# First and third attention: products of 512 constant columns that nobody reads, behind the phases of the delta rule

## What is computed

```python
q, k = l2norm(q), l2norm(k); v = v * beta; kb = k * beta
A = where(tri, 0, -(kb @ k^T))            # per chunk
inv = (I - A)^-1                          # reference: row by row
u, w = inv @ v, inv @ kb
for each chunk:                           # scan, state S
    u_adj = u - w @ S
    out = q @ S + where(strict, 0, q @ k^T) @ u_adj
    S = S + k^T @ u_adj
```

## Time and profile before

| | us |
|---|---|
| median of 3 runs | 5696.86 |
| lowest, highest | 5684.6, 5700.64 |
| profiled execution | 5712.86 |
| its span | 5711.5 |
| PE busy | 4092.1 (72%) |
| DVE busy | 3020.5 (53%) |
| ACT busy | 1912.4 (33%) |
| POOL busy | 816.5 (14%) |
| mean granted clock of PE | 0.761 of 2.4 GHz |

### The profile page before, as it was taken

One profiled execution on the slowest core, in us unless ns is written; L12 is line 12 of the kernel. 1 busy time (PEld: TensorE's weight loads), 2 busy tenths in 40 slices (PEclk: granted clock), 3 DMA queues, 4 the chain that ended last, 5 costly groups with the idle time before them and its releaser, 6 DMA issues.

```text
span 5711.5 us, 93833 instructions
## 1 busy us (share of the span) xinstructions
PE 4092.1 (72%) x39179; PEld 3175.9 (56%) x39228; DVE 3020.5 (53%) x8021; ACT 1912.4 (33%) x4196; POOL 816.5 (14%) x600
## 2 busy tenths in 40 slices
PE   6786969367777877774747668586777777776398
PEld 5674848255555655653536556474444555455277
DVE  4545363425554455556355665656666666665233
ACT  2233231223333333331232332324444555552122
POOL 0000000231111011101610000001212111110444
PEclk7555555588898998885766666668898998897599
DMA  9100000140000000001210000000000000000255
GB/s 271 46 2 1 2 1 2 59 157 1 1 1 1 1 1 1 1 1 36 28 43 2 1 1 2 1 3 1 1 1 1 1 1 1 1 1 17 72 160 143
DMA packets 140856, 152.26 MB, mean 27 GB/s; under 512 B 7809, under 2 KB 128003, under 8 KB 139793
## 3 DMA queue, kind: packets, MB, share of 16 engines
q1 hardware_dynamic: 119024, 128.21, 7.6%
q0 software_dynamic: 21408, 18.05, 1.9%
HBM read 87.38 MB, written 59.76 MB: 26 GB/s over the span
## 4 chain that ended last, share of the span: by engine, by line
PE 50%; DVE 29%; ACT 12%; issue 4%; POOL 2%; DMA 2%; another core or an unknown queue 1%; SPq 0%; DVEq 0%; POOLq 0%; ACTq 0%
PE banks_lane L801 4%; ACT work L3241 4%; PE banks_lane L422 3%; PE banks_lane L3678 2%; PE banks_lane L1881 2%; PE banks_lane L1242 2%; PE banks_lane L809 2%; PE banks_lane L3127 2%; PE banks_lane L935 2%; PE banks_lane L3162 1%; PE banks_lane L3149 1%; ACT work L1975 1%; DVE work L2796 1%; DVE weights L3251 1%
## 5 line engine op out<-in xcount | busy, mean ns | idle before, releaser
L422 PE MATMUL banks_lane<-constants,work 128*128 128x128 f32 x968 | 194.6, 346 | 453.2 <-DVE work L408 208.1
L422 PEld LDWEIGHTS banks_lane<-constants,work 128*128 128x128 f32 x968 | 146.2, 179 | 521.0 <-DVE work L408 195.6
L422 PE MATMUL banks_lane<-constants,weights 128*128 128x128 f32 x596 | 125.3, 347 | 355.7 <-DVE weights L408 93.3
L402 POOL TENSOR_TENSOR weights<-weights,constants 128x4 f32<-128x4 f32 x76 | 78.6, 1034 | 1974.0 <-DVE weights L397 1974.0
L422 PEld LDWEIGHTS banks_lane<-constants,weights 128*128 128x128 f32 x596 | 89.0, 179 | 389.9 <-issue 168.8
L3241 ACT ACTIVATE work<-banks_lane,weights 128x192 f32<-128x192 f32 (+1 forms) x512 | 249.4, 506 | 137.0 <-DVE weights L3338 137.0
L402 POOL TENSOR_TENSOR work<-work,constants 128x4 f32<-128x4 f32 x76 | 77.4, 1019 | 1193.6 <-DVE work L397 1193.6
L3345 POOL TENSOR_TENSOR weights<-weights,constants 128x16 f32<-128x16 f32 x64 | 185.5, 2898 | 377.6 <-DVE weights L3253 377.6
L3334 DVE TENSOR_REDUCE weights<-banks_lane 128x2 f32<-128x384 f32 (+1 forms) x256 | 122.4, 520 | 145.5 <-PE banks_lane L3149 145.5
L2028 DVE TENSOR_REDUCE work<-banks_lane 128x2 f32<-128x512 f32 x256 | 158.8, 683 | 67.6 <-PE banks_lane L1895 67.4
L3162 PE MATMUL banks_lane<-constants,work 128*128 128x128 f32 x896 | 136.1, 298 | 80.8 <-DVE work L3326 43.5
(11 more groups left out here) (773 smaller groups left out, 11034.4 us busy)
## 6 DMA issues: line engine op xcount, KB each, us to landing
work<-experts_dram_l_ffn SPq DMA_DIRECT2D x39, 964.0 KB
room_l_ffn<-work SPq DMA_DIRECT2D x30, 1188.0 KB, 14.2
work<-experts_dram_l_ffn SPq DMA_DIRECT2D x23, 512.0 KB
weights<-weights_dram SPq DMA_DIRECT2D x1, 4833.5 KB, 14.3
work<-room_l_ffn SPq DMA_DIRECT2D x36, 132.0 KB
weights<-weights_dram SPq DMA_DIRECT2D x1, 4112.0 KB, 12.6
weights<-bands_dram SPq DMA_DIRECT2D x1, 4096.0 KB, 13.7
weights<-room_l_ffn SPq DMA_DIRECT2D x26, 132.0 KB
```

The lines of the kernel that those rows point to most:

```text
L402: pool.tensor_tensor(n.rstd, n.rstd, c("neghalf", cols=(0, n.rstd.shape[1])), ALU.pow).then_inc(*u.pool.step(name))
L422: done = pe.transpose(bank[0:rows, t * P:(t + 1) * P], block, c("ident"))
```

## The change

`keep_busy` issues n products of "ident" with "later": 128 rows, 128 weight columns, 512 bfloat16 columns, start and stop set, into a whole bank of the unit's own lane. It increments no semaphore and waits for none. It is called

- at the entry of each unit, 8 times (`FILL_ENTRY`), behind L1062 in the first attention, behind the transpositions to rows in the third (there with a wait for ACT's `v_rows0`, so that b[0] has been read);
- behind each left phase 2 and behind each right phase 3 times; in pair 0 of the first attention 2 more each;
- behind left 5, right 5 and left 6 (L817, L826, L841) 2 times each; behind the transpositions (L834) and right 6 (L848) none;
- behind the values (L935) and the output of each chunk (L1101, L2674) once each.

The bank is b[0], in the third attention's chunks b[3] and b[1]. That makes 1216 products, 672 in the first attention and 544 in the third. Nothing is removed, and no other engine's instructions change. Line numbers of the changed kernel are 6 to 19 higher from there on (L801 becomes L810, L809 L819, L1242 L1261, L935 L949, L1089 L1106, L1099 L1117, L1101 L1119).

```diff
+def keep_busy(pe, masks, place, n):
+    for _ in range(n):
+        pe.matmul(place, masks("ident"), masks("later"), start=True, stop=True)
+
+FILL_LEFT, FILL_RIGHT, FILL_LEFT5, FILL_RIGHT5, FILL_LEFT6, FILL_VALUES, FILL_ENTRY = 2, 3, 2, 2, 2, 1, 8
...
-    def levels_pe(self, pe, u, pair, between):
+    def levels_pe(self, pe, u, pair, between, more=0):
...
             made.then_inc(*u.pe.step(f"left{pair}_{n}"))
             next(between, None)
+            keep_busy(pe, self.masks, b[0][:, :], FILL_LEFT + more)
             yield f"left{pair}_{n}"
...
             made.then_inc(*u.pe.step(f"right{pair}_{n}"))
             next(between, None)
+            keep_busy(pe, self.masks, b[0][:, :], FILL_RIGHT + more)
             yield f"right{pair}_{n}"
...
+        keep_busy(pe, self.masks, b[0][:, :], FILL_LEFT5)
         yield f"left{pair}_5"
...
+        keep_busy(pe, self.masks, b[0][:, :], FILL_RIGHT5)
         yield f"right{pair}_5"
...
+        keep_busy(pe, self.masks, b[0][:, :], FILL_LEFT6)
         yield f"left{pair}_6"
...
 # L0Attn.pe
         pe.matmul(b[3][:, :], w("fuse_hidden"), m.zT).then_inc(*u.pe.step("held"))
+        keep_busy(pe, masks, b[0][:, :], FILL_ENTRY)
...
-            yield from d.levels_pe(pe, u, pair, products)
+            yield from d.levels_pe(pe, u, pair, products, 2 if pair == 0 else 0)
...
                 d.values_pe(pe, u, j).then_inc(*u.pe.step(f"u{chunk}"))
+                keep_busy(pe, masks, b[0][:, :], FILL_VALUES)
                 yield f"u{chunk}"
...
                 made.then_inc(*u.pe.step(f"out{chunk}"))
+                keep_busy(pe, masks, b[0][:, :], FILL_VALUES)
                 yield f"out{chunk}"
...
 # L2Attn.pe
         yield "rows"
+        pe.wait_ge(*u.act.at("v_rows0"))
+        keep_busy(pe, masks, b[0][:, :], FILL_ENTRY)
         yield "norms"
...
                 d.values_pe(pe, u, j).then_inc(*u.pe.step(f"u{chunk}"))
+                keep_busy(pe, masks, b[3][:, :], FILL_VALUES)
...
                 made.then_inc(*u.pe.step(f"out{chunk}"))
+                keep_busy(pe, masks, b[1][:, :], FILL_VALUES)
```

More of the change, by code:

```diff
@@ L1009, in __init__ @@
                       for lane in range(LANES)]
+        for m in self.lanes:
+            m.delta.masks = run.masks
         self.units, self.filters, self.products = units_of(run, ["l0_attn"]), None, None
@@ L1040, in pe @@
     def pe(self, pe, u):
-        m, b, w, c = self.lanes[u.lane], u.banks, self.w, self.c
+        m, b, w, c, masks = self.lanes[u.lane], u.banks, self.w, self.c, self.run.masks
         d = m.delta
```

## The result

The changed kernel takes 5823.53 us (median of 4 runs, 5795.03 to 5838.35) against 5693.7 us before; ratio 1.0225, 95% interval 1.0207 to 1.0244. It is slower by 2.25%, 130 us. Forecast were 5540 us in a range of 5475 to 5790, with 0.23 for slower. The profiled execution has a span of 5837.0 us, 125.5 more than before.

What follows compares the result with a forecast made beforehand. PE was taken to bound the delta rule at half clock; wide products would raise it. Four first-attention rounds at -26.7 (-107) and eight third-attention pairs at -6.1 (-49) sum to -156: 5540 us, range 5475 to 5790.

Steps and rivals of the forecast that it cites:

- I take it that this raises the clock within about a level: Levels: wide products beside small ones (7.7 us beside 11.2, 4.3 beside 5.5) lift the clock and hold it at 2.4 GHz.
- The low time: Low clock at each pair's start: +5.6 us in pair 0, +2.6 in pair 1 per first-attention round; +2.6 per third-attention pair.
- The low prices: A level at the low clock with added products: 18.9 us in pair 0, 9.8 in pair 1.
- The bound of 5632: Upper bound of the likeliest case: one more level low in every pair, +91 us.
- Small and wide products all halve at the high clock: All PE products in both attentions' delta rule: time halves at 2.4 GHz, as the third attention's chunk nearly does.
- levels gave 0.5 back instead of 1.6: Levels at the high clock: pair 0 from 11.2 to 9.6 us, -1.6 each; pair 1 from 5.5, -0.4 each.
- the stretch gave 5.7 and 2.4 for 7.5 and 4.2: 32x32 and 64x64 products closing the inverse: pair 0 from 24.0 us, -7.5; pair 1 from 15.1 to 10.9, -4.2.
- Always high, -34.9 per round: First attention, per round: chunks -15.2, stretch -11.7, pair 0's levels -6.4, pair 1's -1.6, without the low clock at the start.
- 0.22 and 0.43 us a product: Price of one added wide product on PE: 0.22 us at the high clock, 0.43 at the low one.
- the chunks (2.72 for 2.79, 3.47 for 3.66): Lane-chunk at the high clock: first attention 4.69 to 2.79 us, -15.2 per round; third 3.66, -2.9 per pair.
- The one with low chunks after a fall in the stretch: Clock rises in levels, falls in the 64x64 stretch, chunks low: first attention alone 5732, chance 0.10; third too 5862, 0.05.
- The first rival: Levels and 64x64 stretch: the clock does not rise, added products cost 0.43 us each, +437 us, 6134; chance 0.09.

Runs made afterwards that it cites:

- the half rows: The run of 8's kernel with every added product on 64 rows instead of 128, columns and number the same: 6340.91 us, ratio 1.1070.
- the doubled levels: Changed kernel with 4 and 6 instead of 2 and 3 wide products behind each level's left and right phases (pair 0, first attention: 6 and 8): 5782.95 us, 1.0146.
- The run of 8: Changed kernel with 8 more wide products behind the first left phase of every lane and pair: 5709.98 us, ratio 1.0020.
- The kernel with both additions: The run of 8's kernel plus, in the closing stretch, two wide products behind the transpositions and one behind the last 64x64 products: 5708.80 us, ratio 1.0008.
- the best kernel: Kernel before plus, first attention only, 9 wide products ahead of each pair's chunks and one behind each values and out phase: 5677.39 us, ratio 0.9921.
- A run of nine products: Kernel before plus 9 wide products ahead of the first attention's chunks: alone 0.9947, with one behind each values and out phase 0.9921, alone in both attentions 0.9966.
- one of five: The best kernel with 5 instead of 9 wide products ahead of the first attention's chunks: ratio 0.9990.

## Why the prediction was wrong

- **"I take it that this raises the clock within about a level"** is the step that failed. What raises it is right (wide products, 128 rows deep; shown by the half rows and by the doubled levels), and that it then holds in levels, stretch and chunks is right for a section that is up. But between the small ones at 1.2 GHz the eighteen of a level sometimes lift it and sometimes do not: in the first attention pair 0 rose after 45 us in round 1, within a level in rounds 2 and 4, not at all in round 3 (620 to 720 us at 0.50). The run of 8, the only thing added, put the levels up in every pair there and gave back some 115 us. Why one round rises and the next, with the same instructions, does not stays open.
- **The low time was mis-sized.** Per round of the first attention I allowed 5.6 + 2.6 = 8.2 us for it. The three rounds measured average +17.1 us (810.8 against 759.4). With the high prices of the table an always-high round would be -2.0 +2.0 -5.7 -2.4 -15.8 = -23.9; so low stretches cost 41, not 8.2. In the third attention, the same way: +9.9 per pair, -3.9 by high prices, 13.8 where I had 2.6. The low prices (19.0 for 18.9, 10.4 for 9.8) were nearly right; how often they are paid was not. The bound of 5632 allowed one more low level per pair, which is too few by whole sections.
- **"Small and wide products all halve at the high clock"** failed as well. From start to start 32 of the 64x32 kind take 1.73 us low (from 687.63 us on the earlier trace rows to the next row below) and 1.05 high (481.34 to 482.39); 64 of the 32x16 kind in pair 0 take 0.98 low and 0.66 high (403.73 to 404.39). Ahead of the wide products behind 32x16 ones there is an idle time as well, 0.16 us high and 0.33 low. So levels gave 0.5 back instead of 1.6, and cost 0.5 instead of giving 0.4; the stretch gave 5.7 and 2.4 for 7.5 and 4.2. Always high, -34.9 per round was really -23.9. The kernel with both additions has 245.2 us a round, -8; less its own 44 products of 0.22 that is -17.6. Even with the clock up throughout, the forecast was half as large again as the truth, and two thirds of the gain sit in the chunks. The low-clock rows behind these prices, on the timeline of PE in the kernel before:

```profile
356.89 1.05 PE L809 MATMUL banks_lane<-work 32*32 32x16 f32 x64
357.87 1.46 PE L1242 MATMUL banks_lane<-weights 128*64 128x16 f32 x12
...
689.36 1.90 PE L801 MATMUL banks_lane<-weights,work 64*64 64x32 f32 x32
```

They are of the low clock; what they become at the high one stands in no row of the first attention before, and I took the chunk of the third for it.
- **Right**: PE bounds the stretches; 0.22 and 0.43 us a product; the chunks (2.72 for 2.79, 3.47 for 3.66); that levels begin low at the start of a pair (its cause, the waits, is not shown); what DVE and ACT need stays hidden (waits in the high levels stay under a microsecond).
- **The rivals.** The one with low chunks after a fall in the stretch names a place that exists: round 1 and the kernel with the run fall there. Its price (5732, 5862) brackets the measured time, but that is luck: rounds 2 and 4 pass the stretch high, and part of the low time lies in the levels, which it had high (pair 0's of rounds 1 and 3). The first rival (6134, no rise) is of the kind that half the rows gave: 6341, with 256 products more, 110 us at 0.43. The Trainium skill, "TensorE: Matmul & The Clock Gate", Part 1, has the gate set by how busy PE has recently been; 54 and 71 us of a wholly busy PE at 0.50 speak against it as it is put, and I was right not to take it. But the trace of before held a warning that I passed over: in the third attention the 128-row products of the chunks began at 3013.1 us, and PE was still at 0.50 until 3027 us (64x64 products stand among them until 3017 us). The rise needs more than being the right kind of work.

## What to carry on

In this kernel, filling to lift the clock paid only where the work behind it is dense enough to hold the clock by itself and long enough to repay it: put a run, not a sprinkling, directly ahead of such a stretch, and leave stretches of small products alone. Even so the best kernel gained 0.8%. Price the fill at the low clock over a whole section, for that is what it costs where it fails. And before a sum of small gains is trusted, look in the first trace of the change for a state that holds itself: equal code with unequal times (278, 282, 250 us) is its mark.

## What the runs showed of the hardware

- TensorE's clock does not follow its busy share. Busy 71.00 of 71 us at 0.50 with 512-column products on 64 rows; at 1.00 throughout with 49.00 of 49 us and the same kind on 128 rows.
- The same mixture (most of pair 0) stays at 0.50 for 100 us in round 3 (620 to 720 us) and at 1.00 for 65 us in round 2 (390 to 455 us). It takes less to hold the clock than to raise it: the chunks held it without help (1.00 for 12 us, PE busy 10.00 of them), and before the change never rose into it in the first attention.
- A run of nine products, 3.24 us, lifted it in 23 of 24 pairs of the first attention, one of five in 4 of 8.
- What products gain by the high clock differs: 2.0 times for the chunks' 128-row ones (5.4 to 2.72 us a lane-chunk), 1.65 for 64x32, 1.5 for 32x16.
